# Token norms placed further ahead of their transposes, and norms left to an attention run as single steps, in a four-layer transformer kernel

## What is computed

```python
x = x + L0_xattn(LN(x), ctx)      # causal self and cross attention, 16 heads of 16
x = x + L0_ffn(LN(x))             # ternary weights, gelu, 256-1024-256
x = x + L1_xattn(LN(x), ctx)      # cross attention, 16 heads of 16
x = x + L1_ffn(LN(x))             # weights adapted for each batch from 16 of its tokens
x = x + L2_xattn(LN(x), ctx)
x = x + L2_ffn(LN(x))             # four matmuls of ternary weights, silu and gelu
x = x + L3_xattn(LN(x), ctx)
x = x + L3_ffn(LN(x))             # values rounded to 4 bits in blocks of 16
```

```python
def _mha(x, y, ...):
    xn = _ln(x, lnx_g, lnx_b); yn = _ln(y, lny_g, lny_b)
    a = softmax(q(xn) @ k(yn) * D ** -0.5)
    x_out = x + (a @ v(yn)) @ li1_w + li1_b
    h = gelu(_ln(x_out, ln3_g, ln3_b) @ li2_w + li2_b)
    return x_out + h @ li3_w + li3_b
x = _ln(xx, ln1_g, ln1_b)
x = x + _mha(x, x, a1...)         # masked after the softmax
x = _ln(x, ln2_g, ln2_b)
return x + _mha(x, ee, a2...)
```

## Time and profile before

| what | us |
| --- | --- |
| median of three runs | 3705.73 |
| lowest and highest of them | 3694.93, 3719.20 |
| the profiled execution | 3721.88 |
| its span | 3720.1 |
| mean granted clock of TensorE in it | 0.851 |

### The profile page before, as it was taken

One profiled execution on the slowest core, in us unless ns is written; L12 is line 12 of the kernel. 1 busy time (PEld: TensorE's weight loads), 2 busy tenths in 40 slices (PEclk: granted clock), 3 DMA queues, 4 the chain that ended last, 5 costly groups with the idle time before them and its releaser, 6 DMA issues. The chain is left out here.

```text
span 3720.1 us, 44722 instructions
## 1 busy us (share of the span) xinstructions
PE 2878.4 (77%) x16749; PEld 1623.2 (44%) x16756; DVE 2043.9 (55%) x3603; ACT 1434.6 (39%) x1900; POOL 1141.8 (31%) x1007
## 2 busy tenths in 40 slices
PE   4888997758848769999776899777998995787243
PEld 2333333623325434444563344366777773232121
DVE  3445546756625444445765566674454433663687
ACT  1355556326622124445313455432333331565111
POOL 2122322212222125556323688540010111122233
PEclk7699998869968879999876899788999996798555
DMA  5455552035420001111100000001211113553000
GB/s 117 87 108 123 114 115 77 6 86 117 97 64 1 17 3 39 39 42 62 52 12 1 1 1 1 23 1 30 94 49 54 63 42 78 102 117 69 8 9 13
DMA packets 129174, 198.49 MB, mean 53 GB/s; under 512 B 35712, under 2 KB 65920, under 8 KB 128832
## 3 DMA queue, kind: packets, MB, share of 16 engines
q1 hardware_dynamic: 97216, 143.23, 17.0%
q0 software_dynamic: 31744, 52.41, 5.0%
HBM read 130.73 MB, written 64.75 MB: 53 GB/s over the span
## 5 line engine op out<-in xcount | busy, mean ns | idle before, releaser
L2062 DVE TENSOR_REDUCE L_mx<-bank_t 128x2 f32<-128x1024 f32 (+3 forms) x512 | 562.9, 1122 | 474.7 <-PE bank_t L1871 290.2
L2268 ACT ACTIVATE L_P<-bank_t 128x1024 f32<-128x1024 f32 (+2 forms) x512 | 477.8, 947 | 446.1 <-PE bank_t L1885 295.0
L2062 DVE TENSOR_REDUCE L2a_mx<-bank_t 128x2 f32<-128x1024 f32 x256 | 311.8, 1224 | 420.5 <-PE bank_t L1848 419.6
L2268 ACT ACTIVATE L2a_P<-bank_t 128x1024 f32<-128x1024 f32 x256 | 261.6, 1023 | 303.1 <-PE bank_t L1860 302.6
L1871 PE MATMUL bank_t<-L_KS,L_QS 48*128 48x512 f32 (+2 forms) x1024 | 259.3, 509 | 114.1 <-DMA L_QS<-L_spill_q_halves 92.2
L1848 PE MATMUL bank_t<-L2a_QK 32*128 32x512 f32 x1536 | 258.0, 454 | 82.2 <-DVE L2a_mx L2062 47.1
L1885 PE MATMUL bank_t<-L_QS,L_KS 50*128 50x512 f32 (+2 forms) x1024 | 236.6, 465 | 92.1 <-DVE L_mx L2062 69.5
L1916 PE MATMUL bank_o<-L_P,L_V 128*32 128x512 f32 (+3 forms) x2048 | 280.7, 623 | 3.1 <-ACT xn L2275 1.8
L1871 PEld LDWEIGHTS bank_t<-L_KS,L_QS 48*128 48x128 f32 x1024 | 107.1, 208 | 361.7 <-issue 262.4
L1856 PE MATMUL bank_t<-L2a_QK 32*128 32x512 f32 x1536 | 259.9, 447 | 0.0
L1848 PEld LDWEIGHTS bank_t<-L2a_QK 32*128 32x128 f32 x1536 | 139.6, 201 | 250.8 <-ACT L2a_P L2268 114.5
(11 more groups left out here) (431 smaller groups left out, 6046.2 us busy)
## 6 DMA issues: line engine op xcount, KB each, us to landing
L_KS<-L_spill_k_halves SPq DMA_DIRECT2D x192, 128.0 KB, 4.5
L_QS<-L_spill_q_halves SPq DMA_DIRECT2D x192, 128.0 KB, 5.0
L_spill_raw<-xn POOLq DMA_DIRECT2D x64, 256.0 KB, 2.4
L2g_raw<-in_L_ffn_h_blocks SPq DMA_DIRECT2D x32, 512.0 KB, 3.8
L_spill_k_halves<-L_hi SPq DMA_DIRECT2D x32, 256.0 KB, 2.0
L_spill_k_halves<-L_lo SPq DMA_DIRECT2D x32, 256.0 KB, 2.3
L_spill_q_halves<-L_hi SPq DMA_DIRECT2D x32, 256.0 KB, 5.0
L_spill_q_halves<-L_lo SPq DMA_DIRECT2D x32, 256.0 KB, 5.2
```

What stands on the lines that cost most here:

```text
L2062: e.tensor_reduce(neg, s.tile[:, :, 0:n_keys], AX.X, ALU.max, negate=True).then_inc(sem(s.done), 1)
L2268: e.activation(s.at.Pr[s.pb][:, :, q0:S], s.tile[:, :, q0:S], ACT.Exp, scale=s.at.scale).then_inc(sem(s.exp), 1)
```

## The change

1. Stats is split into Stats (bn_stats and bn_aggr) and Root (the twelve small instructions). The norms of L2_entry become lists of four steps: stats of two tiles, stats of two tiles, root, normalise.
2. Side takes a list as one item. In a feed-forward one tick runs the whole list, as before; what is left for an attention is handed over as single steps, each a chore. The attention now inserts its own preparation ahead of the first left-over chore that may be put off (`side.free`, `queue_up`).
3. LazyNorm's normalise is issued one unit ahead of its turns.
4. In split_ffn the turns of batches 1 and 2 and the norm of 2 move later in the hidden tiles, and the turns of batch 3 move between the tiles of output(1). The side list's ticks in hidden(1) start at m = 6.
5. L0's feed-forward has a pause of 7 in place of 2 between LazyNorm's normalise and its turns.
6. In L2_entry a1's turns of a batch wait until the following batch is written and its pause is 1; for a2 the context's fetches, norms and turns and the first batches' steps stand in another order, with longer pauses before the turns.

```diff
+Root = namedtuple("Root", "t0 t1 after done")
...
-    def put(self, step, ready=lambda: True, held=False):
-        self.items.append((ready, step, held))
+    def put(self, steps, ready=lambda: True, held=False):
+        self.items.append((ready, steps if isinstance(steps, list) else [steps], held))
...
     def rest(self):
-        steps = [item[1] for item in self.items]
+        steps = [step for item in self.items for step in item[1]]
+        self.free = [step for item in self.items if not item[2] for step in item[1][:1]]
...
+            def queue_up(steps):
+
+                i = next((i for i, c in enumerate(chores) if side is not None and c in side.free), len(chores))
+                chores[i:i] = steps
+
...
+                if norm is not None and un.n + st.n + 1 < len(units):
+                    then = units[un.n + st.n + 1]
+                    if then.u == 0 and then.j == 0:
+                        new += norm.steps(then.b, misc)[:1]
...
-                                chores += new
+                                queue_up(new)
...
-                    if b > 1 or b == 1 and m > 3:
+                    if b > 1 or b == 1 and m > 5:
                         side.tick()
...
-                between[0] = {2: turns(1)[:1], 4: turns(1)[1:], 5: [lambda: norm(2)]}
+                between[0] = {3: turns(1)[:1], 5: turns(1)[1:], 6: [lambda: norm(2)]}
...
-                between[1] = {1: turns(2)[:1], 3: turns(2)[1:], 4: [lambda: add_bias(0)]}
-                between[2] = {0: [lambda: norm(3, tail.raw_free)], 1: [lambda: add_bias(2)], 5: turns(3)[:1],
-                              7: turns(3)[1:]}
+                between[1] = {4: [lambda: add_bias(0)], 5: turns(2)[:1], 6: turns(2)[1:]}
+                between[2] = {0: [lambda: norm(3, tail.raw_free)], 1: [lambda: add_bias(2)]}
...
-                        output(b - 1, behind, ring, f.W2)
+                        output(b - 1, behind, ring, f.W2, dict(zip((1, 3), turns(3))) if b == 2 else {})
...
-                side.pause(2, held=True)
+                side.pause(7, held=True)
...
-                    pause(2, held=True)
+                    pause(1, held=True)
                     for step in turns:
-                        put(step, held=True)
+                        put(step, written(min(b + 1, B - 1)), held=True)
...
-            put(fetch0)
+            put(fetch0, lambda: E.turned(2))
             pause(1)
             put(context0)
-            pause(1)
             _, normal, affine, inner, turns = batches[0]
             put(normal, written(0), held=True)
+            put(affine, held=True)
             for step in turns0:
                 put(step, held=True)
-            put(affine)
-            pause(2)
+            pause(1)
             put(inner)
-            pause(2, held=True)
+            pause(4, held=True)
...
-            put(fetch1, lambda: E.turned_last())
+            put(fetch1, lambda: E.turned(B - 1))
             pause(1, held=True)
             put(context1, held=True)
             put(inner, held=True)
+            pause(2, held=True)
+            for step in turns1:
+                put(step, held=True)
             pause(1, held=True)
-            for step in [*turns1, *turns]:
+            for step in turns:
```

More of the change, by code:

```diff
@@ L343, in normal @@
                         self.stats(b)
-                    state["n"] = normalise([(xn[:, 0, i, :], X[:, TB * b + i, :], TB * b + i) for i in range(TB)],
+                    self.normal[b] = normalise([(xn[:, 0, i, :], X[:, TB * b + i, :], TB * b + i) for i in range(TB)],
                                            [self.e_stats[b], xn_free[0]])
@@ L354, in turn_part @@
                     self.ready[b] = (self.ready[b] or []) + [e_e]
-                return [normal] + [lambda k=k: turn_part(k) for k in range(KC)]
+                turns = [lambda k=k: turn_part(k) for k in range(KC)]
+                if b in self.begun:
+                    return turns
+                self.begun.add(b)
+                return [normal] + turns
         def make_stacks(tag, D, keep, n_units, mode="full", kept=()):
@@ L816, in attention @@
                 finished.add(un.n)
-                chores += after
+                queue_up(after)
             while pending:
@@ L991, in hidden, with output @@
                 return e_h
-            def output(b, e_h, ring, W2, tiles=range(TB)):
-                for t in tiles:
+            def output(b, e_h, ring, W2, between=()):
+                for t in range(TB):
+                    if t in between:
+                        between[t]()
                     at, tile_at = TB * b + t, slice(t * P, t * P + P)
@@ L1017, in main @@
                 if f.entry is not None:
-                    f.entry.weights_free, f.entry.turned_last = f.weights_free, f.turned_last
+                    f.entry.weights_free, f.entry.turned = f.weights_free, f.turned
                 side.ring = ring = Banks(ALL.aps[:7])
@@ L1048, in split_ffn @@
             f.entry = None
-            f.steps, f.main, f.written, f.turned_last = steps, main, 0, lambda: len(e_x[B - 1]) == KC
+            f.steps, f.main, f.written, f.turned = steps, main, 0, lambda b: len(e_x[b]) == KC
             return f
@@ L1228, in affine, with to_inner @@
                     state["y"] = add_rows(v, b_, [e_m])
-                def inner():
-                    e = norm_stats(lambda t: Y[:, t, :], lambda t: state["y"], TB * b, TB * b + TB)
+                def to_inner():
                     state["x"] = normalise([(xn[:, 0, i, :], Y[:, t, :], t) for i, t in enumerate(tiles(b))],
-                                           [e, xn_free[0], *(E.side.busy or ())])
+                                           [state["root"], xn_free[0], *(E.side.busy or ())])
+                inner = [*statistics(lambda t: Y[:, t, :], lambda t: state["y"]), to_inner]
                 def turned(k):
```

47 lines of the change are left out of this document (30 added, 17 removed).

## The result

The changed kernel takes 3695.6 us (median of 20 runs, 3679.7 to 3721.6), the one before 3711.7 (20 runs, 3694.9 to 3721.9). The ratio is 0.9963, with a 95% interval of 0.9945 to 0.9981: 16 us off, where 81 were forecast, and outside the stated range of 3580 to 3685. The profiled execution took 3705.9 us, its span 3703.9, at a mean granted clock of 0.852 against 0.851 before.

The account below looks back on a forecast made before the run. TensorE, busy 77%, was taken to set the pace while waiting for VectorE's normalises and row-maxima. Terms 29 + 31 + 4 + 7 + 6 + 4 = 81 us off the 3705.7 us median gave 3625 us; range 3580 to 3685.

Parts of the forecast that it names:

- L1's feed-forward, 29 us: L1's feed-forward: moving two batches' turns removes two 14 us waits and slow restarts, leaving about 3 us; gain 29 us.
- a1's start, 17 us: Start of L2 attention a1: norms in pieces gain 14 us, plus 3 of a 5.04 us wait before it.
- the 85% I had let VectorE be busy: Starts of a1 and a2: with split norms VectorE is busy 85% of the time, a chosen value; 14 us each.
- a2's start, 14 us: Start of L2 attention a2: norms in pieces cut a stretch of 59 us to 45, a gain of 14 us.
- the forecast keeps 81: Attention starts: split roots meeting POOL sums could give back 8 us, leaving 73; not deducted, as the trace already had blocking.
- The feed-forwards of L0, a1 and a2, 4, 7 and 6 us: Feed-forwards of L0, a1 and a2: moved norms and turns cut PE's waits, gaining 4, 7 and 6 us.
- LazyNorm, 4 us with a bound of -3: D = 16 attentions: earlier normalise starts some 4 batch boundaries 1 us sooner, 4 us; bound -3 if it delays a row-maximum.
- Slower: D = 16 attentions: early normalise and POOL row add delay K and Q halves, 18.7 us per boundary, up to 3793; chance 0.04.
- Only the stage with idle VectorE pays: L1's feed-forward gains 25 to 29 us, attentions 10, the rest 0 to 10; total 35 to 50; chance 0.22.
- The bound does not move: Feed-forwards: late turns make hidden tiles wait equally long instead; gain under 30 us, about 3690; chance 0.07.
- The signs: Checks: L1's 14 us waits gone; a1 and a2 clocks above 0.85, no L2062 wait over 3 us; xn waits 70 or less.
- the third rival: Whole kernel, "everything returns": all moved waits (89 us) and the two attentions (40) are gained, giving 3577 us; chance 0.14.

Follow-up runs that it names:

- e1_no_early: The changed kernel with LazyNorm's normalise back at its old place, one unit later, all else as changed: 3661.1 us against 3712.5 for the kernel before, ratio 0.9865.

## Why the prediction was wrong, point by point

- *L1's feed-forward, 29 us.* Right by its own steps: both 14 us waits gone, one of 3.35 us left where 3 was worked out, 28.6 us in the profile and 40 (26 to 52) in the run with this part alone.
- *a1's start, 17 us.* Right in size, in part by luck: 15.0 us. The way was another than the 85% I had let VectorE be busy: from exp 1 to 14 it did 40.6 us of work before and does 25.7 now (66% of the time), since some of the norms' pieces went on to later ticks. That stretch gained 19.6 us, and the next 46 exps gave 4.6 back.
- *a2's start, 14 us.* Wrong. The step that failed is "Of the 5.6 us ... a root of 2.4", and with it "the forecast keeps 81, since the trace has the blocking in it already". In place of 14 us gained a2 lost 9.9. Its first 24 exps gained 14.4 us, as forecast; the 32 after them lost 24.6, with PE busy 14.7 us longer at a clock of 0.88 and idle 10 us longer. The three roots took 6.5, 4.9 and 5.0 us in place of 2.3, 3.1 and 4.7. That is 6.3 us in all, so the longer roots alone are not the 24; the rest came with the lower clock and with a norm in a stretch that had none before. The forecast also took one blocked instruction for all that the trace of before showed. That trace holds a chain with three at the end of a2, where a root took 10.25 us:

```profile
2367.94 2.19 DVE L2009 SCALAR_TENSOR_TENSOR nw<-nw 128x4 f32<-128x4 f32 x1
...
2370.37 2.19 DVE L2007 TENSOR_TENSOR nw<-nw 128x4 f32<-128x4 f32 x1
...
2372.79 2.19 DVE L2013 SCALAR_TENSOR_TENSOR nw<-nw 128x4 f32<-128x4 f32 x1
```

  The Trainium skill, "SBUF — State Buffer", section "Who interferes with whom", by which a VectorE instruction with two SBUF inputs, or one in a two-port mode, and a POOL instruction that reads SBUF exclude each other, had been weighed at 8 us given back. The traces agree with it (2.19 to 2.22 us for an instruction of 0.16), and the loss is larger.
- *The feed-forwards of L0, a1 and a2, 4, 7 and 6 us.* 3.4, 8.1 and 5.7 in the profile, but only a2's is well shown: 151.9 to 154.1 us in the five kernels with the new orders, 156.1 to 158.4 in the others. L0's stretch took 180.1 to 185.8 us with them and 180.8 to 191.3 without, so its 3.4 is not shown. a1's took 216.7 to 220.8 against 222.4 to 227.2, a gain, but of a size that was met by luck: the waits for xn there fell only from 23.4 to 21.3 us, and one of 10.21 is new. The orders alone brought 6 us where the three terms have 17.
- *LazyNorm, 4 us with a bound of -3.* Wrong, and most of the miss. The step that failed is the term itself, four batch boundaries that start 1 us earlier, with one delayed row-maximum (-3) as its lower bound: the normalise was priced at its own 1.38 us. It costs 34 us (the changed kernel against e1_no_early) to 45 us (alone). I priced neither the meeting with L_lo on POOL, of which the earlier trace rows held the price (0.69 against 2.88), nor that one step more moves every projection of its unit by two ticks.
- *The rivals.* "Slower" named the place, the three 16-head attentions, the normalise, and POOL's row add; its price (18.7 us waits for K and Q halves) was not what came: those waits fell from 92.2 to 80.3 us. "Only the stage with idle VectorE pays" had 35 to 50 us, still too high, and a1's start paid too. "The bound does not move" (a gain under 30, about 3690) has the total that came, by luck: its mechanism, hidden tiles that wait as long as the transposes did, is not what L1's 28.6 us show. A time within 1% of before had been given 0.10.
- *The signs.* L1's feed-forward and a1's start (0.87, no wait over 3 us for the row-maximum) did what was named. a2's start did not: 0.74 over 54 us and waits of 5.3 and 5.2 us. The waits of tile xn came to 89.8 us, not 70 or less. And one sign of being wrong came, the wait over 8 us in front of a context's transposes (10.21).
- *The sum.* With LazyNorm at -38.6 and a2 at -9.9 the terms give 28.6 + 15.0 - 9.9 + 3.4 + 8.1 + 5.7 - 38.6 = 12, against 16.2 between the two spans. Two slips in the working changed nothing: L1's upper bound adds up to 32 and not 33, and the third rival's 3577 lies just outside the range that is said to take it in.

## What to carry to other kernels

Cost a moved step by what POOL does beside it at its new tick, and by what its place in a list moves along; here its own length, 1.38 us of 34 to 45, was the smallest part. A norm in pieces paid in a1 (14 to 18 us) and not in a2, where POOL's sums stretch a chain of small instructions from 2.3 to 8.5 us and the last pieces come late; look at both before you split. And take a change of six parts apart: here a1's turns and a1's pieces carried all of the gain, and the early normalise took two thirds of it back.

## What the hardware showed

The same 468 matmuls of L0's attention (64th to 104th exp) took 75 to 92 us, at a mean granted clock of 1.00 to 0.83 and with PE busy 87 to 93% of the time. The eight kernels without early normalise or shift had 0.94 to 1.00; moving a few projections by two ticks, earlier or later, gave 0.88 both times. Instructions on 128 x 4 values took 2.19 us beside POOL sums of 2.4 us, over 13 times their 0.16, and three in a chain of twelve did so.
